# A slot gather moved behind the fourth run, node rows loaded whole, and two of six one-hots moved to VectorE

## The reference

```python
h = jnp.maximum(_layernorm(x, axis=-1), 0.0)
x = x + _L0_gnn_ref(h, edge_weight, src, dst, ...)

# inside _L0_gnn_ref
def _weighted_mean_agg(ft, w, src, dst, n_nodes):
    m = ft[src] * w[:, None]
    msum = jax.ops.segment_sum(m, dst, num_segments=n_nodes)
    wsum = jax.ops.segment_sum(w, dst, num_segments=n_nodes)
    ...                                        # msum / wsum, 0 where wsum is 0
neigh1 = _weighted_mean_agg(feat, w, src, dst, n)
neigh2 = _weighted_mean_agg(feat, w, dst, src, n)
hn = jnp.concatenate([neigh1 @ W1.T, neigh2 @ W2.T], axis=1)
gi = hn @ w_ih.T + b_ih
gh = feat @ w_hh.T + b_hh
r, z = sigmoid(i_r + h_r), sigmoid(i_z + h_z)
nn_ = jnp.tanh(i_n + r * h_n)
return nn_ + z * (feat - nn_)
```

## Time and profile before

| | |
|---|---|
| Median of 3 executions | 10,286.35 us (10,271.16 to 10,287.65) |
| The profiled execution, its own time | 10,286.65 us |
| Its span, first to last instruction | 10,284.9 us |
| Share of the span that TensorE is busy | 86% |
| VectorE, ScalarE, GpSimd | 57%, 57%, 52% |
| Mean granted TensorE clock | 0.947 of full speed |
| The sums of layer 1 | about 124 to 3,564 us |
| Its node stage | about 3,564 to 3,804 us |

### The profile page before, as it was taken

One profiled execution on the slowest core, in us unless ns is written; L12 is line 12 of the kernel. 1 busy time (PEld: TensorE's weight loads), 2 busy tenths in 40 slices (PEclk: granted clock), 3 DMA queues, 4 the chain that ended last, 5 costly groups with the idle time before them and its releaser, 6 DMA issues. The chain is left out here.

```text
span 10284.9 us, 240162 instructions
## 1 busy us (share of the span) xinstructions
PE 8865.8 (86%) x58497; PEld 7104.9 (69%) x58498; DVE 5868.4 (57%) x12333; ACT 5835.7 (57%) x15502; POOL 5342.0 (52%) x5246
## 2 busy tenths in 40 slices
PE   5888888888888859999899699999998499999998
PEld 5888888888888737777566466666665376666666
DVE  6666666666666537777311455555555455555555
ACT  5666666766666535444200467767765455555555
POOL 5666666666666400000000277777775277777775
PEclk8999999999999979999899799999999799999999
DMA  3111111111111102222354344444443122222222
GB/s 120 38 36 38 36 38 36 37 37 36 38 36 37 34 21 106 112 112 112 136 190 157 122 118 118 118 118 118 118 118 97 50 73 73 73 72 72 72 73 69
DMA packets 466279, 827.25 MB, mean 80 GB/s; under 512 B 160873, under 2 KB 333102, under 8 KB 446127
## 3 DMA queue, kind: packets, MB, share of 16 engines
q0 software_dynamic: 193536, 455.41, 16.1%
q1 hardware_dynamic: 272430, 368.67, 10.4%
HBM read 672.16 MB, written 151.40 MB: 80 GB/s over the span
## 5 line engine op out<-in xcount | busy, mean ns | idle before, releaser
L1688 POOL DMA_INDIRECT x<-table,p_gidx x1632 | 1547.2, 948 | 2458.0 <-ACT p_gidx L1725 2004.0
L634 POOL DMA_INDIRECT g_G<-table,g_runs x1776 | 2061.0, 1160 | 547.5 <-issue 540.2
L2189 POOL DMA_INDIRECT c_G<-table,c_gidx x1632 | 1554.8, 953 | 505.7 <-issue 493.4
L771 PE MATMUL g_ps_cell<-g_kw,g_loh 128*128 128x98 f32 x9472 | 1280.3, 281 | 27.6 <-DVE g_kw L687 27.6
L771 PEld LDWEIGHTS g_ps_cell<-g_kw,g_loh 128*128 128x128 f32 x9472 | 1215.3, 201 | 28.0 <-DVE g_kw L687 28.0
L782 PE MATMUL g_ps_rev<-g_hrow,g_AT 128*128 128x129 f32 x7252 | 1077.5, 286 | 95.5 <-ACT g_AT L748 66.4
L1779 PE MATMUL p_ps_sum<-x 128*96 128x256 f32 x3264 | 896.6, 398 | 157.9 <-DVE hid L1714 140.7
L782 PEld LDWEIGHTS g_ps_rev<-g_hrow,g_AT 128*128 128x128 f32 x7252 | 928.2, 196 | 130.7 <-ACT g_AT L748 94.3
L804 PE MATMUL g_ps_run<-g_Gw,g_roh 128*128 128x130 f32 x3552 | 577.8, 311 | 397.6 <-ACT g_Gw L727 397.6
L1714 DVE TENSOR_TENSOR hid<-hid,p_ps_sum 96x256 f32 x1632 | 678.0, 415 | 376.6 <-DVE hid L1714 373.2
L1779 PEld LDWEIGHTS p_ps_sum<-x 128*96 128x96 f32 x3264 | 469.5, 163 | 559.2 <-DVE hid L1714 204.4
(11 more groups left out here) (346 smaller groups left out, 17417.5 us busy)
## 6 DMA issues: line engine op xcount, KB each, us to landing
adj_save<-a_A SPq DMA_DIRECT2D x74, 1568.0 KB, 5.1
a_A<-adj_save SPq DMA_DIRECT2D x74, 1568.0 KB, 6.6
c_ed<-in_edge_dram SPq DMA_DIRECT2D x1632, 25.0 KB
g_G<-table,g_runs POOLq DMA_INDIRECT x1776
x<-table,p_gidx POOLq DMA_INDIRECT x1632
p_lhs<-in_edge_dram SPq DMA_DIRECT2D x1632, 16.0 KB
c_G<-table,c_gidx POOLq DMA_INDIRECT x1632
table<-m_rows SPq DMA_DIRECT2D x17, 384.0 KB, 2.5
```

What stands on the lines that cost most here:

```text
L634: g.indirect_dma_start(G[:, e % GR, q, 0:D], None, table, bass.IndirectOffsetOnAxis(ap=runs[:, n % 2, 0, RQ * e + q:RQ * e + q + 1], axis= ...
L771: last = pe.matmul(ps_cell[q % 2][:, r * KEYS:(r + 1) * KEYS], loh[:, b, cell, :], kw[:, b, cell, :], start=True, stop=True)
L1688: g.indirect_dma_start(G[:, H * b + q, :], None, table2, bass.IndirectOffsetOnAxis(ap=gidx[:, b, q:q + 1], axis=0)).then_inc(gathered[b], 16)
L2189: g.indirect_dma_start(G[:, H * b + q, :], None, table, bass.IndirectOffsetOnAxis(ap=gidx[:, b, q:q + 1], axis=0)).then_inc(gathered[b], 16)
```

## The change

GpSimd's slot gather moves from the head of a batch to behind the four gathers of run 3; its wait on `rev_made` moves with it. The one-hots of runs 1 and 4 are made by VectorE, as four comparisons each with the result in one step; ScalarE keeps those of runs 0, 2, 3 and 5, at the halves where they stood. `weigh_run` of runs 1 and 4 gets the wait on `run_made` that stood in `make_run_oh`; `sum_run` of those runs waits for VectorE (`compared`); the load of the run numbers waits for the runs to be summed, not only weighed. In the node stage `xin` and `hin` hold all 49 tiles, every chunk has its own semaphore, and SyncE's 26 loads have no waits.

```diff
-OH_AT = {0: 0, 2: 1, 5: 2, 8: 3, 10: 4, 13: 5}
+OH_AT = {0: 0, 5: 2, 8: 3, 13: 5}
+VECTOR_OH_AT = {3: 1, 11: 4}
...
                             if not (isinstance(n, int) and n < 2):
-                                sp.wait_ge(weighted, RPB * (n - 1))
+                                sp.wait_ge(run_made, RPB * (n - 1))
...
                         for n in range(NBATCH):
-                            if n >= 2:
-                                g.wait_ge(rev_made, TGS * (n - 1))
-                            g.indirect_dma_start(hrow[:, n % 2, 0:D], None, table,
-                                                 bass.IndirectOffsetOnAxis(ap=dst_tab[:, n % 2, n // 2:n // 2 + 1], axis=0)).then_inc(gathered[n % 2], 16)
                             g.wait_ge(runs_in[n % 2], 16 * (n // 2 + 1))
                             for e in range(RPB):
...
+                                if e == RPB - GR:
+                                    if n >= 2:
+                                        g.wait_ge(rev_made, TGS * (n - 1))
+                                    g.indirect_dma_start(hrow[:, n % 2, 0:D], None, table,
+                                                         bass.IndirectOffsetOnAxis(ap=dst_tab[:, n % 2, n // 2:n // 2 + 1], axis=0)
+                                                         ).then_inc(gathered[n % 2], 16)
...
+                        def compare_run(n, s, iteration, bb):
+
+                            if s not in VECTOR_OH_AT or not known(n):
+                                return
+                            e = VECTOR_OH_AT[s]
+                            m = RPB * n + e
+                            v.wait_ge(runs_in[bb], 16 * (iteration + 1))
+                            if not (isinstance(m, int) and m < 2):
+                                v.wait_ge(run_made, m - 1)
+                            for q in range(RQ):
+                                last = v.tensor_scalar(roh[:, e % 2, q, :], iota, runs[:, bb, 1, RQ * e + q:RQ * e + q + 1].bitcast(F32), None, ALU.is_equal)
+                            last.then_inc(compared, 1)
...
-                            s.wait_ge(away, m + 1)
+                            s.wait_ge(away, 4 * n + (0, 0, 1, 2, 0, 3)[e] + 1)
...
+                            if e in (1, 4) and not (isinstance(n, int) and n == 0 and e < 2):
+                                s.wait_ge(run_made, RPB * n + e - 1)
...
+                            if e in (1, 4):
+                                pe.wait_ge(compared, 2 * n + (e == 4) + 1)
                             pe.wait_ge(weighted, m + 1)
...
-                xin = sb("u_xin", [P, 2, CT, D], F32, ctx)
-                hin = sb("u_hin", [P, 2, CT, D], F32, ctx)
+                xin = sb("u_xin", [P, NTQ, D], F32, ctx)
+                hin = sb("u_hin", [P, NTQ, D], F32, ctx)
...
                         for c in range(NCH):
-                            if c >= 2:
-                                sp.wait_ge(turned, c - 1)
-                            sp.dma_start(hin[:, c % 2, 0:count(c), :], tiles(table)[:, tiles_in(c), :]).then_inc(h_in[c % 2], 16)
-                            if c >= 2:
-                                sp.wait_ge(added, c - 1)
-                            sp.dma_start(xin[:, c % 2, 0:count(c), :], a["x"][:, tiles_in(c), :]).then_inc(x_in[c % 2], 16)
+                            sp.dma_start(hin[:, tiles_in(c), :], tiles(table)[:, tiles_in(c), :]).then_inc(h_in[c], 16)
+                            if c >= 1:
+                                sp.dma_start(xin[:, tiles_in(c - 1), :], a["x"][:, tiles_in(c - 1), :]).then_inc(x_in[c - 1], 16)
+                        sp.dma_start(xin[:, tiles_in(NCH - 1), :], a["x"][:, tiles_in(NCH - 1), :]).then_inc(x_in[NCH - 1], 16)
```

More of the change, by code:

```diff
@@ L584, in stage_gru_sums @@
                 turned, at_ready, rev_made, rev_added, applied = (sem(f"g_{k}") for k in ("turned", "at_ready", "rev_made", "rev_added", "applied"))
-                away, weighted, run_made, added = (sem(f"g_{k}") for k in ("away", "weighted", "run_made", "added"))
+                away, compared, weighted, run_made, added = (sem(f"g_{k}") for k in ("away", "compared", "weighted", "run_made", "added"))
                 gathered = [sem(f"g_gathered{b}") for b in range(2)]
@@ L698, in body @@
                                 add_run(n_then, s)
+                                compare_run(n_then, s, i if cc >= 2 or bb == 1 else i - 1, n_parity[0])
                                 if known(n):
@@ L702, in body @@
                                 add_run(n_then, s + 1)
+                                compare_run(n_then, s + 1, i if cc >= 2 or bb == 1 else i - 1, n_parity[0])
                         over_bodies(v, body)
@@ L868, in stage_gru_nodes @@
                 loaded, folded, ready = sem("u_loaded"), sem("u_folded"), sem("u_ready")
-                x_in = [sem(f"u_x_in{b}") for b in range(2)]
-                h_in = [sem(f"u_h_in{b}") for b in range(2)]
+                x_in = [sem(f"u_x_in{c}") for c in range(NCH)]
+                h_in = [sem(f"u_h_in{c}") for c in range(NCH)]
                 rest_in, stats_in = sem("u_rest_in"), sem("u_stats_in")
@@ L906, in turn @@
                             pe.wait_ge(means_ready, 2 * c + 2)
-                            pe.wait_ge(h_in[c % 2], 16 * (c // 2 + 1))
+                            pe.wait_ge(h_in[c], 16)
                             if c >= 1:
@@ L911, in turn @@
                                 for t in range(count(c)):
-                                    rows = nodes[:, c % 2, k, t, :] if k < 2 else hin[:, c % 2, t, :]
+                                    rows = nodes[:, c % 2, k, t, :] if k < 2 else hin[:, CT * c + t, :]
                                     last = pe.transpose(ps_turn[k][:, t * P:(t + 1) * P], rows, ident[:, :])
@@ L992, in add @@
                             v.wait_ge(turned_back, c + 1)
-                            v.wait_ge(x_in[c % 2], 16 * (c // 2 + 1))
-                            v.tensor_tensor(x[:, tiles_in(c), :].rearrange("p t d -> p (t d)"), xin[:, c % 2, 0:count(c), :].rearrange("p t d -> p (t d)"),
+                            v.wait_ge(x_in[c], 16)
+                            v.tensor_tensor(x[:, tiles_in(c), :].rearrange("p t d -> p (t d)"), xin[:, tiles_in(c), :].rearrange("p t d -> p (t d)"),
                                             ps_back[:, 0:cols(c)], ALU.add).then_inc(added, 1)
```

## The result

The changed kernel took 9,727.58 us (median of 4 runs, 9,724.11 to 9,743.78), the kernel before, beside it on the same chip, 10,278.76 (4 runs, 10,268.54 to 10,287.65). The ratio is 0.9467, 95% interval 0.9451 to 0.9484: 551 us less. The forecast was 9,694 with a range from 9,590 to 9,835. The time lies in the range, 34 us above the forecast. That closeness is partly luck: the forecast took the wrong engine for the bound, which made its batch too long, and left out stops at the ends of loops, which made it too short, as the experiments show.

A forecast was written before the change was run, and what follows sets the result against it. It took TensorE's waits, in the sums for a chain through GpSimd's slot gather, as the time to gain, and GpSimd's queue as the next bound. 10,286.65 − 497 (sums) − 96 (node stage) = 9,694 us, range 9,590 to 9,835.

The forecast's parts named there:

- The wait: In the sums, GpSimd stands 10 us per batch with the slot gather at its queue's head; forecast to go.
- the hole: In the sums, TensorE idles 5.47 us per batch ahead of a run, for ScalarE's weighing; forecast to go.
- the low clock: Behind that idle time TensorE runs at its lower clock, costing 1.54 us more per batch; forecast to go.
- So GpSimd becomes the bound by a hair, at 39.0: Sums after the change: 25 gathers of 1.56 us make GpSimd's queue 39.0 us per batch, just above TensorE.
- What is late next: Which queue sets the sums' pace afterwards: TensorE at 37.2 to 39.1 us per batch, or GpSimd at 39.0.
- rival B: In the sums TensorE stays the bound at 38.0 us per batch; 9,608 us in all; chance 0.17.
- rival A: The forecast itself: GpSimd's queue bounds the sums at 38.6 to 40 us per batch; 9,636 to 9,752; chance 0.55.
- Rival C: In the sums VectorE's comparisons hold GpSimd up, 41 to 43 us per batch; 9,831 at 41.1; chance 0.20.
- while VectorE makes `koh` or `kw`: In the sums, GpSimd's gathers are held up during these VectorE instructions, 1.56 us each in a dense stretch.
- Worth 0: Relieving ScalarE of two one-hots, 3.8 us per batch, gains 0, at most 0.4 us, as ScalarE isn't the bound.
- D: In the sums the slot gather or a row gather still waits; only the node stage gains; 10,190 us; chance 0.04.
- E: In the sums many short waits keep TensorE at its lower clock, slower than before, up to 11,487; chance 0.03.

The follow-up runs named there:

- e6: Changed kernel with one more gather per batch, whose rows nobody reads, behind the slot gather; 9,732.0 us.
- e9: e7 with one more gather per batch, whose rows nobody reads, behind the slot gather; 9,640.9 us.
- e5: Changed kernel with ScalarE's and VectorE's programs of the sums written out without loops; 9,593.5 us.
- e11: Changed kernel without its one-hot part, with ScalarE's and VectorE's programs of the sums written out without loops; 9,591.0 us.
- e7: Changed kernel with 40 increments of an unused semaphore ahead of ScalarE's loop of the sums; 9,633.0 us.
- e8: Changed kernel without its one-hot part, so slot gather and node stage alone; 9,637.0 us.
- e4: Changed kernel with ScalarE's program of the sums written out for all batches instead of a loop; 9,634.1 us.
- e1: Kernel before with only the slot gather moved behind run 3; 9,733.0 us.
- e3: Kernel before with only the node stage's edit, its rows loaded whole; 10,187.3 us.

## Why the prediction was right or wrong

**Slot gather.** The wait, the hole and the low clock went as it said, and the new place cost nothing. "So GpSimd becomes the bound by a hair, at 39.0" is the step that failed. Alone, this part gave 543 us and a distance of 38.5, more than the 497 forecast for it together with the one-hots. The prediction took 1.56 us per gather from one stretch of 14. Over the stage of the changed kernel a gather takes 1.191 + 0.305, and a batch 24 × 1.496 + 1.27 = 37.2 us. The stretch had been picked where VectorE's long instructions follow each other, which is denser than a batch is on average; the mean of the whole stage, 1.46, which the prediction had beside it, was nearer. e6 and e9 showed the slack directly.

**What is late next** was TensorE, at 37.98 us. That is rival B, to which the prediction gave 0.17, with its 38.0 and its 9,608 us; e5 and e11 came to 9,594 and 9,591. The prediction's own sign of B was there too: between 200 and 2,850 us GpSimd waited for `weighted` 103 times in 67 batches. So the time of the changed kernel fell into the range of rival A by neither A's mechanism nor B's alone, but by B's and the stops. The bounds "37.2 to 39.1" for TensorE held. Two slips in the prediction's figures change nothing: 38.6 us per batch would be 9,651 us and not 9,636, and the 0.43 for the turn back stands in no row of rows 11, though it is what the changed kernel shows (3206.70 to 3207.13).

**One-hots.** For ScalarE, VectorE, TensorE's wait and GpSimd the costs came out as predicted: in e7 against e8 the whole part is −4 us, inside the scatter. Rival C fell. The timeline of the changed kernel shows a gather beside the comparisons and one beside `kw`:

```profile
1519.18 0.94 POOL L631 DMA_INDIRECT g_G<-table,g_runs  x1 [0.30 <-issue]
1519.53 0.90 DVE L691 TENSOR_SCALAR g_roh<-numbers,g_runs 128x128 f32<-128x128 f32 x4
...
1522.43 0.96 DVE L703 TENSOR_TENSOR g_kw<-g_koh,w_tab 128x784 f32<-128x784 bf16 x1
1522.49 1.72 POOL L631 DMA_INDIRECT g_G<-table,g_runs  x1 [0.30 <-issue]
```

It is so throughout. Counted in the timelines of e5_act_dve_straight between 500 and 2,500 us, 105 gathers overlap a comparison and no `kw`, and none takes over 0.95 us. The 422 that overlap a `kw` take 1.66 on average, and each over 1.0. Beside `koh` alone none takes over 0.96, so the prediction's "while VectorE makes `koh` or `kw`" holds for `kw`; some that meet `loh` take up to 1.3. With the comparisons the mean gather was even shorter, 1,179 ns in e7 against 1,227 in e8: in the same stretch, of 1,297 gathers each, 64 were lengthened beside `loh` in e7 and 238 in e8, and nearly as many met a `kw` (395 and 415).

"Worth 0" failed all the same: the part costs 91 us in the changed kernel. None of it is work. It shortened ScalarE's loop by 12 instructions and moved it up by 33, and a turn's end went from nothing seen to 4.4 us. The prediction named no such term.

**The stops of VectorE** were in the trace of before, once per turn, and the prediction's cost of a batch left them out: in the hole they cost nothing, and with the hole gone, 41 us (e4 to e5). In numbers: 38.0 for TensorE, about 0.5 for VectorE's stops, about 1.3 for ScalarE's, 39.8 in all. The forecast had 39.2 by another way; a bound 1.0 to 1.2 us too high stood in for stops of 1.8 us.

**Load of run numbers:** 0, as predicted; e11 and e5 differ in it and not in time.

**Node stage.** 9.47 us per chunk against 9.5, no load waited for, and 96 us from e1 to e8, as forecast. The trace has 99.4, e3 alone 88 ± 18.

**Rivals D and E:** the slot gather waits for nothing, no gather's wait holds TensorE's runs up, and the clock is at 0.99. Where TensorE waits 2.1 us once in two batches, it stays near its higher level.

## What to carry to other kernels

When a hole is closed, everything that happened inside it comes on the path: list what the other engines do during the hole, above all their stops at loop ends ("issue", once per turn), before taking the rest of the period as the new one. An edit that changes only the number of instructions ahead of or within a loop can move the time by 1%; where such an edit "costs" something that no work explains, compare the packets of the instruction queue and put a few idle instructions ahead of the loop before judging the edit. A duration for a queue's pace is to be taken over a whole period, not from its densest stretch.

## What the hardware showed that was not expected

- The end of a turn of ScalarE's loop: no stop seen at 622 to 920 or 629 to 915, 4.4 us at 589 to 875 and again at 256 further. On the path it is worth 95 us in about 35 turns, 2.7 us each.
- Writing loops out did not mean more packets of instructions in every case. On the queue that ScalarE's and VectorE's programs use there were 408 in the changed kernel and 238 in e7_pad40, 290 with ScalarE's loop written out (e4) and 178 with VectorE's too (e5). TensorE's own queue went from 74 packets to 254 (of 16 KB) when its loop was written out, without any change in the distance of batches.
- VectorE's comparisons did not hold GpSimd's gathers up (0.95 us at most beside them), nor did `koh`; `kw` (f32 out of bf16) lengthened every gather that it met, from 0.94 to 1.66 us on average. So the two engines affect each other there without any semaphore between them.
